# A graph network's edge loop: one own-computed edge tile per lap in place of three, shorter address lists, and the window ramp in SBUF

## The chip, the cores and the metric

The kernel runs on one core of a Trainium2 chip. The metric is the device time of one execution in microseconds (us). Of the kernel before it is 1872.18 us, the median of three runs that lie between 1870.85 and 1880.07.

## The reference, cut to what matters

A message-passing layer over 12500 nodes of 64 features and 200000 edges of 32 features. The edges are sorted by destination node.

```python
msg_in = jnp.concatenate([nodes[row], nodes[col], edge_features], axis=-1)
messages = relu(msg_in @ mW1 + mb1) @ mW2 + mb2
aggregated = jax.ops.segment_sum(messages, col, num_segments=nodes.shape[0])
upd_in = jnp.concatenate([nodes, aggregated], axis=-1)
upd = relu(upd_in @ uW1 + ub1) @ uW2 + ub2
out = layernorm(nodes + upd)
```

Here `row` is `src` (random) and `col` is `dst` (sorted). The first layer of the message network is linear ahead of its relu, so its three parts can be computed apart and added: one part from the source node, one from the destination node, one from the edge.

## The kernel before, in words

**Tables.** The kernel first multiplies all node rows with the source part of `mW1` and writes the result to DRAM as `src_table`, then does the same for the destination part (`dst_table`). GpSimd waits until `src_table` is stored before its first gather.

**The edge loop.** The edges are cut into tiles of 128, four tiles to a group, eight groups to a lap: 32 tiles a lap, 49 laps, of which the last has 7 groups. In all there are 391 groups. For each group g:

- GpSimd (`gather`, L305 to L317) fetches rows of `src_table` with one indirect DMA for each tile into `ag`. It may run at most eight groups ahead of the compute engines: it waits for `s_pre` of group g - 8.
- SP loads a window of 96 rows of `dst_table` (L329) and the edges' features (L323).
- VectorE makes a one-hot matrix `oh` (L402): it compares a ramp `iota` of 96 numbers with each edge's place in the window, for four tiles at once. Both inputs are broadcast to 128 x 384.
- TensorE transposes it (L338), ScalarE copies it to SBUF (L383), and TensorE multiplies destination window and edge features with it (L353).
- VectorE adds the gathered source part (`add_source`, L416), ScalarE applies the relu (L394), TensorE adds the rows of one destination up (L368, L372), and VectorE adds the window into the sums (`add_window`, L433 and L434).

**Own tiles.** Some tiles of a lap are not gathered. `OWN_OF` says how many in each of the eight groups of a lap: one each in groups 0, 2 and 5, so 3 of 32. For these the kernel fetches the feature columns of the source nodes itself from `xc`, which lies in SBUF: one copy of 64 x 4 bytes for each edge, at an address that is read from `own_list` into a register (L282). The 384 columns of a lap are spread evenly over its eight groups, `OWN_N` = 48 in each: `OWN_DVE` = 20 by VectorE (L290, in `own_columns`), the other 28 by ScalarE (L302). `DVE_AHEAD` and `ACT_AHEAD` = 12 say how many addresses each engine reads into registers ahead of its `add_source` or its relu; the rest is read behind it. TensorE then multiplies the own tile with `w_src` (L357), and the relu of such a group is in two parts (L391, L392). The copies of one lap are for the tiles of the next. The first lap has no own tiles.

**Order on VectorE in group g:** one-hot of group g + 2, register reads, `add_source` of g, register reads, `add_window` of g - 2, own copies, then in some groups a piece of the update.

**The update.** From lap 26 on (`UPD_LAP`), one chunk of 512 nodes a lap goes through the update network and the layer norm, in pieces between the groups (L749 to L841). Two chunks are left for after the last lap, and end the kernel. Three of these pieces read two SBUF tensors in one VectorE instruction: L770, L802 and L828.

Of the kernel before, what the change touches and what calls it, by code (L numbers as in the profile page):

```python
# [9 lines left out]
P = 128  # L10
# [12 lines left out]
WIN = 96  # L23
# [13 lines left out]
UPD_LAP = ITERS - CHUNKS + TAIL  # L37
TB = 4
TSTEPS = -(-BLOCKS // TB)
OWN_OF = (1, 0, 1, 0, 0, 1, 0, 0)  # L40
OWN_TILES = sum(OWN_OF)
OWN = OWN_TILES * P
OWN_N = OWN // UNROLL
OWN_DVE = 20
DVE_AHEAD = 12
ACT_AHEAD = 12
LIST = OWN // 2
XPARTS = 8
XP = NODES // XPARTS
# [7 lines left out]
def build(nc, x_rows, x_t, src_first, src_all, src_own, dst_groups, dst_tiles, edge_t,  # L57
# [12 lines left out]
    with ctx:  # L70
        def sb(name, shape, dt=f32):
            return ctx.enter_context(nc.sbuf_tensor(name, shape, dt))
# [19 lines left out]
        ident_bf = sb("ident_bf", [P, P], bf16)  # L92
        eps = sb("eps", [P, 1])
        iota_i = sb("iota_i", [P, WIN], i32)
        ones_bf = sb("ones_bf", [P, P], bf16)
        w_src = sb("w_src", [P, DH])
        b1_rows = sb("b1_rows", [P, DH])
# [11 lines left out]
        xc = sb("xc", [P, NODES])  # L109
# [42 lines left out]

        banks = [ctx.enter_context(nc.psum_tensor(f"bank{i}", [P, 512], f32)) for i in range(8)]
        ps_h, ps_o, ps_a = banks[0:2], banks[2:4], banks[4:6]
        iota = banks[6][:, 0:WIN]


        s_first = sem("s_first")
# [85 lines left out]
        def gathered_tiles(k):  # L244

            return TPG - OWN_OF[k]

        def has_own(k, lap):

            return OWN_OF[k] > 0 and not (isinstance(lap, int) and lap == 0)  # L250

# [25 lines left out]
        def own_places(et, k, lap, a, b):  # L277

            if a == b or isinstance(lap, int) and lap == ITERS - 1:
                return []  # L280
            at = k * OWN_N
            return nc.values_load_multi_w_load_instructions(  # L282
                own_list[0:1, at + a:at + b], engines=(et,), min_val=x_at, max_val=x_at + 4 * (N_NODES - 1),
                skip_runtime_bounds_check_because="the address of a node's column in xc")[1]

        def own_columns(k, a, places, copy, s_done):

            at = k * OWN_N + a
            for n, place in enumerate(places):
                done = copy(own_x[:, at + n:at + n + 1].bitcast(u8),  # L290
                            xc[0:D, :].bitcast(u8)[:, ds(place - x_at, 4)])
            if places:
                done.then_inc(s_done, 1)
# [5 lines left out]
        def own_columns_act(k, places):  # L299

            def copy(to, of):
                return nc.scalar.activation(to, of, ACT.Copy)  # L302
            own_columns(k, OWN_DVE, places, copy, s_own_act)

# [37 lines left out]
        def hidden(pe, g, k, lap):  # L342
# [7 lines left out]
            own = gathered_tiles(k) if has_own(k, lap) else TPG  # L350
            before_k = sum(OWN_OF[:k])
            for j in range(TPG):
# [24 lines left out]
        def copy_oh(g, k):  # L377

            act = nc.scalar
            q, r = k % 2, k % RING  # L380
            wait(act, s_oht_mm, g + 1)
            wait(act, s_h, g - RING + 1)
            act.activation(picks[0:WIN, r, :], ps_o[q][0:WIN, :], ACT.Copy).then_inc(s_oht, 1)  # L383

        def relu(g, k, lap):
            act = nc.scalar
            q = k % 2
            wait(act, s_pre, g + 1)
            if has_own(k, lap):
                at = gathered_tiles(k) * DH  # L390
                act.activation(hid[:, q, at:], ps_h[q][:, at:], ACT.Relu)  # L391
                act.activation(hid[:, q, 0:at], hid[:, q, 0:at], ACT.Relu).then_inc(s_relu, 1)  # L392
                return
            act.activation(hid[:, q, :], hid[:, q, :], ACT.Relu).then_inc(s_relu, 1)  # L394

        def one_hot(g, k):

            dve = nc.vector
            r = k % RING
            wait(dve, s_agg, g - RING + 1)  # L400
            grid = [P, TPG, WIN]
            dve.tensor_tensor(oh[:, r, :].rearrange("p (j w) -> p j w", w=WIN),  # L402
                              iota[:, None, :].to_broadcast(grid),
                              rel[:, ds(g * TPG, TPG)][:, :, None].to_broadcast(grid),
                              ALU.is_equal).then_inc(s_oh, 1)

        def add_source(g, k, lap):

            dve = nc.vector
            q = k % 2  # L410
            missing = G_END * TPG - T_END if isinstance(g, int) and g == G_END - 1 else 0
            wait(dve, s_gathered[k], gathered_of(k, lap) - 16 * missing)
            wait(dve, s_h, g + 1)
            wait(dve, s_agg, g - 1)
            w = (gathered_tiles(k) if has_own(k, lap) else TPG) * DH
            dve.tensor_tensor(hid[:, q, 0:w], ps_h[q][:, 0:w], ag[:, k, 0:w], ALU.add).then_inc(s_pre, 1)  # L416
# [131 lines left out]
        def exists(g):  # L548

            return not isinstance(g, int) or g < G_END  # L550
# [270 lines left out]
        def dve_normalize(c, v=None):  # L821
            dve = nc.vector
            y = blocks(rows_of(c))
            rstd, _, _, std = stats(c, v)
            dve.wait_ge(s_std, c + 1)
            dve.reciprocal(rstd, std).then_inc(s_rstd, 1)
            dve.wait_ge(s_rstd, c + 1)
            dve.tensor_tensor(y, y, rstd[:, :, None].to_broadcast([P, filled(c), D]), ALU.mult  # L828
                              ).then_inc(s_norm, 1)
# [167 lines left out]
        def _(act):  # L997
# [11 lines left out]
            def windowed():  # L1009
                dst_table_stored(act)  # L1010
                copy_oh(0, 0)

                def lap(i, c):
                    for k in range(UNROLL):
                        g = i * UNROLL + k
                        own_listed(act, k, i)
                        if exists(g + 1):
                            copy_oh(g + 1, (k + 1) % UNROLL)
                        places = own_places(ET.Activation, k, i, OWN_DVE, OWN_DVE + ACT_AHEAD)
                        if exists(g):  # L1020
                            relu(g, k, i)
                        places += own_places(ET.Activation, k, i, OWN_DVE + ACT_AHEAD, OWN_N)
                        own_columns_act(k, places)
                        if before(c) and k == 0:
                            act_square(c - 1)
                        elif before(c) and k == 2:
                            act_deviation(c - 1)
                        elif before(c) and k == 4:
                            act_store(c - 1)
                        elif c is not None and k == 5:  # L1030
                            act_relu(c)

                def finish(c):
                    act_square(c)
                    act_deviation(c)
                    act_store(c)
                laps(act, lap, open_update, finish, act_chunks)
# [10 lines left out]
        def _(dve):  # L1048
# [7 lines left out]
            dve.memset(ones_bf[:, :], 1.0)  # L1056
            dve.memset(src_idx[:, TILES:], 0).then_inc(s_const, 1)
            dve.wait_ge(s_iota, 3)
            dve.tensor_copy(iota, iota_i[:, :])
            dve.tensor_copy(trash_f[:, :], trash_i[:, :])  # L1060
            dve.tensor_copy(lag_f[:, :], lag_i[:, :]).then_inc(s_iotaf, 1)
            dve.wait_ge(s_ident, 2)
# [40 lines left out]
            def windowed():  # L1103
# [9 lines left out]
                def lap(i, c):  # L1113
# [4 lines left out]
                    for k in range(UNROLL):  # L1118
                        g = i * UNROLL + k
                        own_listed(dve, k, i)  # L1120
                        if exists(g + 2):
                            one_hot(g + 2, (k + 2) % UNROLL)
                        places = own_places(ET.DVE, k, i, 0, DVE_AHEAD)
                        if exists(g):
                            add_source(g, k, i)
                        places += own_places(ET.DVE, k, i, DVE_AHEAD, OWN_DVE)
                        if not (isinstance(g, int) and g < 2):
                            add_window(g - 2, (k - 2) % UNROLL, bases[k])
                        own_columns_dve(k, places)
                        if before(c) and k == 1:  # L1130
                            dve_variance(c - 1)
                        elif before(c) and k == 3:
                            dve_normalize(c - 1)
                        if c is not None and k == 1:
                            dve_c2(c)
                        elif c is not None and k == 3:
                            dve_stack(c)
                        elif c is not None and k == 7:
                            dve_center(c)
# [105 lines left out]
```

## Time and profile before

| what | value |
|---|---|
| profiled execution, its own time | 1872.18 us |
| its span, first to last instruction | 1870.4 us |
| median of three runs | 1872.18 us |
| gathers on GpSimd | 1419 |
| one-hots, groups | 391 |
| own copies on VectorE / ScalarE | 7680 / 10752 |
| own tiles | 144 |
| busy share PE / VectorE / ScalarE / GpSimd | 77% / 74% / 82% / 72% |

Busy shares are means over the whole span. What matters is which engine never waits for another. GpSimd's issue gap between gathers is not counted as busy. Start times are counted from the start of the span. The profiled execution is the one whose time equals the median, 1.8 us above its span.

### The profile page before, as it was taken

The page shows a single profiled execution, that of the slowest core. Times are in us where ns is not written, and L with a number is a line of the kernel's source. Part 1 is how long each engine was busy: PE and PEld are TensorE (multiplying, and loading weights), DVE is VectorE, ACT ScalarE, POOL GpSimd, SP SyncE. Part 2 cuts the span into 40 slices and gives each one's busy share as a digit, 9 for nine tenths or more (in the row PEclk, how much of TensorE's full clock was granted, in tenths as well). Part 3 has the DMA queues.
Part 4 walks back from the last instruction along what each step waited for, and adds up shares of the span by engine and source line. Part 5 has one row for each costly group of instructions (what it writes and reads, how often), then busy time and mean ns, then how long its engine had stood idle before and what let it go on. Part 6 is the DMA issues. An engine that isn't in the chain of part 4 may idle for free.

```text
span 1870.4 us, 55266 instructions
## 1 busy us (share of the span) xinstructions
PE 1437.6 (77%) x10368; PEld 1287.0 (69%) x10368; DVE 1381.8 (74%) x9522; ACT 1529.9 (82%) x11781; POOL 1347.6 (72%) x1432
## 2 busy tenths in 40 slices
PE   6677778778777878777777777777777777777776
PEld 6666677677666767766776777666666666676665
DVE  3488777777777777777777778777778778877885
ACT  3399988888888888888888888888888888888884
POOL 1677777777777777777777777777777777777771
PEclk8899887887878787788788778888778878887888
DMA  9933323332323333333332332332233323332331
GB/s 209 263 93 87 88 78 83 86 80 80 86 80 81 83 84 80 83 83 81 81 79 80 81 82 80 80 84 80 79 81 84 81 78 81 85 80 77 84 82 30
DMA packets 170541, 165.24 MB, mean 88 GB/s; under 512 B 70442, under 2 KB 134418, under 8 KB 170402
## 3 DMA queue, kind: packets, MB, share of 16 engines
q0 software_dynamic: 45408, 93.09, 19.1%
q1 hardware_dynamic: 111394, 64.42, 12.5%
q10 hardware_dynamic: 13698, 7.28, 1.8%
q8 instruction: 14, 0.23, 0.1%
q14 instruction: 27, 0.22, 0.0%
HBM read 148.25 MB, written 16.39 MB: 88 GB/s over the span
## 4 chain that ended last, share of the span: by engine, by line
POOL 35%; ACT 16%; issue 16%; PE 12%; DVE 10%; DMA 4%; ACTq 4%; DVEq 3%; POOLq 1%; SPq 0%
POOL ag L314 35%; ACT own_x L302 12%; PE bank L353 5%; ACTq L282 3%; DVE own_x L290 3%; DVE hid L416 2%; PE bank L368 2%; PE bank L749 2%; DMA src_table<-ag 2%; PE bank L762 1%; ACT hid L394 1%; DVEq L282 1%; ACT picks L383 1%; DMA dst_table<-hid 1%; DVE oh L402 1%
## 5 line engine op out<-in xcount | busy, mean ns | idle before, releaser
L314 POOL DMA_INDIRECT ag<-src_table,slot_idx x1419 | 1341.1, 945 | 481.1 <-issue 420.4
L302 ACT ACTIVATE own_x<-xc 64x4 uint8 x10752 | 1064.7, 190 | 101.5 <-issue 101.0
L353 PE MATMUL bank<-picked,picks 128*128 128x128 f32 x3128 | 548.0, 330 | 217.7 <-ACT picks L383 208.5
L353 PEld LDWEIGHTS bank<-picked,picks 128*128 128x128 f32 x3128 | 474.2, 232 | 250.8 <-ACT picks L383 159.5
L290 DVE COPY own_x<-xc 64x4 uint8 x7680 | 606.6, 190 | 12.0
L368 PE MATMUL bank<-oh,hid 128*128 128x96 f32 x3128 | 528.8, 324 | 24.7 <-DVE xc L434 23.8
L368 PEld LDWEIGHTS bank<-oh,hid 128*128 128x128 f32 x3128 | 483.7, 236 | 57.9 <-ACT hid L394 21.0
L416 DVE TENSOR_TENSOR hid<-bank,ag 128x512 f32<-128x512 f32 (+1 forms) x391 | 249.9, 639 | 290.7 <-DMA ag<-src_table,slot_idx 144.2
L402 DVE TENSOR_TENSOR oh<-bank,rel 128x384 f32<-128x384 f32 x391 | 217.9, 557 | 55.5 <-issue 28.7
L338 PE MATMUL bank<-ident_bf,oh 128*96 128x128 bf16 x1564 | 178.4, 244 | 88.2 <-DVE oh L402 86.1
L383 ACT ACTIVATE picks<-bank 96x512 f32<-96x512 f32 x391 | 224.7, 575 | 24.3 <-DMA dst_table<-picks 22.8
L394 ACT ACTIVATE hid<-hid 128x512 f32<-128x512 f32 x247 | 154.3, 625 | 100.2 <-DVE hid L416 100.2
L338 PEld LDWEIGHTS bank<-ident_bf,oh 128*96 128x96 bf16 x1564 | 132.3, 141 | 140.2 <-DVE oh L402 104.9
L372 PE MATMUL bank<-oh,ones_bf 128*128 128x96 bf16 x1564 | 150.0, 224 | 0.0
L433 DVE TENSOR_TENSOR agg_t<-bank,agg_t 128x96 f32 x391 | 100.6, 257 | 61.7 <-issue 32.5
L372 PEld LDWEIGHTS bank<-oh,ones_bf 128*128 128x128 bf16 x1564 | 138.3, 119 | 1.0
L434 DVE TENSOR_TENSOR xc<-bank,xc 64x96 f32 x391 | 102.2, 261 | 5.4
L391 ACT ACTIVATE hid<-bank 128x128 f32<-128x128 f32 x144 | 38.4, 267 | 64.3 <-DVE hid L416 59.6
L357 PE MATMUL bank<-w_src,own_x 64*128 64x128 f32 x288 | 84.9, 382 | 0.0
L392 ACT ACTIVATE hid<-hid 128x384 f32<-128x384 f32 x144 | 74.1, 514 | 0.0
L357 PEld LDWEIGHTS bank<-w_src,own_x 64*128 64x128 f32 x288 | 52.1, 226 | 21.9 <-issue 9.8
L762 PE MATMUL bank<-u,dst_i 128*128 128x64 f32 x196 | 29.1, 295 | 46.9 <-ACT dst_i L786 46.9
(62 smaller groups left out, 414.5 us busy)
## 6 DMA issues: line engine op xcount, KB each, us to landing
picks<-edge_t SPq DMA_DIRECT2D x391, 64.0 KB
ag<-src_table,slot_idx POOLq DMA_INDIRECT x1419
picked<-dst_table SPq DMA_DIRECT2D x391, 48.0 KB
src_table<-ag SPq DMA_DIRECT2D x25, 256.0 KB, 4.1
dst_table<-picks SPq DMA_DIRECT2D x17, 256.0 KB, 4.4
xc<-x_t ACTq DMA_DIRECT2D x8, 400.0 KB, 16.1
resid<-x_rows SPq DMA_DIRECT2D x24, 128.0 KB
out<-resid ACTq DMA_DIRECT2D x24, 128.0 KB
```

The lines of the kernel that those rows point to most:

```text
L290: done = copy(own_x[:, at + n:at + n + 1].bitcast(u8), xc[0:D, :].bitcast(u8)[:, ds(place - x_at, 4)])
L302: return nc.scalar.activation(to, of, ACT.Copy)
L314: pool.indirect_dma_start(out=ag[:, k, j * DH:(j + 1) * DH], out_offset=None, in_=src_table, in_offset=bass.IndirectOffsetOnAxis(ap=slot_i ...
L338: last = nc.tensor.matmul(ps_o[q][0:WIN, j * P:(j + 1) * P], half[:, j * WIN:(j + 1) * WIN], ident_bf[:, :], start=True, stop=True)
L353: last = nc.tensor.matmul(ps_h[q][:, j * DH:(j + 1) * DH], picks[:, r, j * P:(j + 1) * P], picked[:, r, :], start=True, stop=j < own)
L357: last = nc.tensor.matmul(ps_h[q][:, j * DH:(j + 1) * DH], own_x[:, (before_k + j - own) * P:(before_k + j - own + 1) * P], w_src[0:D, :], ...
L368: nc.tensor.matmul(ps_a[q][:, 0:WIN], hid[:, q, j * DH:(j + 1) * DH], oh[:, r, j * WIN:(j + 1) * WIN], start=(j == 0), stop=(j == TPG - 1))
L372: last = nc.tensor.matmul(ps_a[q][:, WIN:2 * WIN], ones_bf[:, :], half[:, j * WIN:(j + 1) * WIN], start=(j == 0), stop=(j == TPG - 1))
L383: act.activation(picks[0:WIN, r, :], ps_o[q][0:WIN, :], ACT.Copy).then_inc(s_oht, 1)
L394: act.activation(hid[:, q, :], hid[:, q, :], ACT.Relu).then_inc(s_relu, 1)
L402: dve.tensor_tensor(oh[:, r, :].rearrange("p (j w) -> p j w", w=WIN), iota[:, None, :].to_broadcast(grid), rel[:, ds(g * TPG, TPG)][:, :, ...
L416: dve.tensor_tensor(hid[:, q, 0:w], ps_h[q][:, 0:w], ag[:, k, 0:w], ALU.add).then_inc(s_pre, 1)
```

## The change

Own tiles are one a lap (in group 0) and not three. A lap's own list is then 128 edges, 16 for each group: eight on VectorE and eight on ScalarE, all of whose addresses are read ahead. The ramp `iota` of the one-hot lies in SBUF, where before it lay in a PSUM bank. The `list(...)` around the register reads changes no instruction.

```diff
-OWN_OF = (1, 0, 1, 0, 0, 1, 0, 0)
+OWN_OF = (1, 0, 0, 0, 0, 0, 0, 0)
 OWN_TILES = sum(OWN_OF)
 OWN = OWN_TILES * P
 OWN_N = OWN // UNROLL
-OWN_DVE = 20
-DVE_AHEAD = 12
-ACT_AHEAD = 12
+OWN_DVE = 8
+DVE_AHEAD = 8
+ACT_AHEAD = 8
...
+        iota = sb("iota", [P, WIN])
...
-        iota = banks[6][:, 0:WIN]
...
-            return nc.values_load_multi_w_load_instructions(
+            return list(nc.values_load_multi_w_load_instructions(
...
-            dve.tensor_copy(iota, iota_i[:, :])
+            dve.tensor_copy(iota[:, :], iota_i[:, :])
```

## Rows read from the trace of the kernel before

**Rows 1.** The page's busy times by engine: us, share of span, instructions.

```profile
PE 1437.6 (77%) x10368; PEld 1287.0 (69%) x10368; DVE 1381.8 (74%) x9522; ACT 1529.9 (82%) x11781; POOL 1347.6 (72%) x1432
```

**Rows 2.** The page's chain that ended last, by engine.

```profile
POOL 35%; ACT 16%; issue 16%; PE 12%; DVE 10%; DMA 4%; ACTq 4%; DVEq 3%; POOLq 1%; SPq 0%
```

**Rows 3.** All gathers, those from 57.6 to 999 us (ns min/median/max, starts), their waits.

```profile
L314 POOL DMA_INDIRECT ag<-src_table,slot_idx x1419: 940/944/1147, 56.3 to 1828.7; - x178
...
L314 POOL DMA_INDIRECT ag<-src_table,slot_idx x754: 940/944/961, 57.7 to 997.9; - x189
...
POOL ag L314 <- issue: 420.4, 1379, 0.3
```

**Rows 4.** Timeline, early gathers and VectorE's first own copies: start, duration in us.

```profile
57.70 0.94 POOL L314 DMA_INDIRECT ag<-src_table,slot_idx  x1 [0.30 <-issue]
58.95 0.95 POOL L314 DMA_INDIRECT ag<-src_table,slot_idx  x1 [0.30 <-issue]
...
90.24 0.90 DVE L290 COPY own_x<-xc 64x4 uint8 x11
```

**Rows 5.** VectorE's longest waits, 400 to 800 us, then 1100 to 1500 us: total, times, longest.

```profile
DVE hid L416 <- DMA ag<-src_table,slot_idx: 70.3, 75, 2.0
...
DVE hid L416 <- PE bank L353: 38.6, 19, 3.5
```

**Rows 6.** Costliest groups that the change touches: count, busy us, mean ns, idle before.

```profile
L302 ACT ACTIVATE own_x<-xc 64x4 uint8 x10752 | 1064.7, 190 | 101.5 <-issue 101.0
L290 DVE COPY own_x<-xc 64x4 uint8 x7680 | 606.6, 190 | 12.0
...
L357 PE MATMUL bank<-w_src,own_x 64*128 64x128 f32 x288 | 84.9, 382 | 0.0
```

**Rows 7.** Timeline around group 105: its last gather, its work on VectorE, group 106.

```profile
538.37 0.94 POOL L314 DMA_INDIRECT ag<-src_table,slot_idx  x1 [0.30 <-issue]
...
540.88 0.69 DVE L416 TENSOR_TENSOR hid<-bank,ag 128x512 f32<-128x512 f32 x1 [0.34 <-DMA ag<-src_table,slot_idx]
541.71 0.26 DVE L433 TENSOR_TENSOR agg_t<-bank,agg_t 128x96 f32 x1
...
542.11 0.94 POOL L314 DMA_INDIRECT ag<-src_table,slot_idx  x1 [0.30 <-issue]
542.27 1.56 DVE L290 COPY own_x<-xc 64x4 uint8 x20
...
543.87 0.56 DVE L402 TENSOR_TENSOR oh<-bank,rel 128x384 f32<-128x384 f32 x1
544.60 0.56 DVE L416 TENSOR_TENSOR hid<-bank,ag 128x384 f32<-128x384 f32 x1 [0.18 <-DMA ag<-src_table,slot_idx]
```

**Rows 8.** Timeline at 1136 us: a two-input SBUF instruction, a gather, the next gather.

```profile
1136.38 0.43 DVE L828 TENSOR_TENSOR resid<-resid,stat 128x256 f32 x1 [0.16 <-DVE stat L826]
1136.48 1.14 POOL L314 DMA_INDIRECT ag<-src_table,slot_idx  x1 [0.30 <-issue]
...
1137.93 0.94 POOL L314 DMA_INDIRECT ag<-src_table,slot_idx  x1 [0.30 <-issue]
```

**Rows 9.** Timeline at 1270 us: the same pair of kinds.

```profile
1270.16 0.42 DVE L802 TENSOR_TENSOR resid<-resid,stat 128x256 f32 x1
1270.35 1.06 POOL L314 DMA_INDIRECT ag<-src_table,slot_idx  x1 [0.30 <-issue]
```

**Rows 10.** Timeline at 1081 us: the same pair of kinds, the gather first.

```profile
1081.51 0.94 POOL L314 DMA_INDIRECT ag<-src_table,slot_idx  x1 [0.31 <-issue]
1081.54 0.43 DVE L802 TENSOR_TENSOR resid<-resid,stat 128x256 f32 x1
```

**Rows 11.** Timeline at the end: last gather, `add_source` of the last group, last issued store.

```profile
1828.71 0.94 POOL L314 DMA_INDIRECT ag<-src_table,slot_idx  x1 [0.30 <-issue]
...
1849.23 0.69 DVE L416 TENSOR_TENSOR hid<-bank,ag 128x512 f32<-128x512 f32 x1 [1.19 <-PE bank L353]
...
1867.11 0.38 ACTq L841 DMA_DIRECT2D out<-resid  x1
```

**Rows 12.** Granted TensorE clock near the end: window, length, PE busy, clock, DMA share, GB/s.

```profile
1855.00:1860.00 5.00, 4.49 (x8) 0.66 0.11 26
```

More of the change, by code:

```diff
@@ L281, in own_places @@
             at = k * OWN_N
-            return nc.values_load_multi_w_load_instructions(
+            return list(nc.values_load_multi_w_load_instructions(
                 own_list[0:1, at + a:at + b], engines=(et,), min_val=x_at, max_val=x_at + 4 * (N_NODES - 1),
-                skip_runtime_bounds_check_because="the address of a node's column in xc")[1]
+                skip_runtime_bounds_check_because="the address of a node's column in xc")[1])
         def own_columns(k, a, places, copy, s_done):
```

## The prediction

> **What bounds the kernel now.** I read the page's busy times first [rows 1]. By them ScalarE, with 82%, looks like the bound and GpSimd, with 72%, like the least loaded. The page's chain of work says something else: GpSimd has the largest part of it, 35%, ahead of ScalarE's 16% [rows 2]. The gathers settle it. From 57.7 to 997.9 us there are 754 of them [rows 3], so 753 intervals of 940.2 / 753 = 1.249 us: 0.94 us of work and 0.30 us in which GpSimd waits for nothing that the profile shows. That "issue" gap stands before 1379 of the 1419 gathers and is never longer than 0.3 us [rows 3]. Over the whole kernel the mean is (1828.7 - 56.3) / 1418 = 1.250 us. So GpSimd never stops between its first gather and its last: the stream of gathers is a rod of 1772 us, and the kernel is the time ahead of it (56.3), the rod, and what comes after the last start (1870.4 - 1828.7 = 41.7).
>
> The other engines are near the bound without being it. In the first half VectorE's `add_source` waits for gathered rows, 75 times between 400 and 800 us. In the second half, where the update is mixed in, its longest wait is for TensorE and the gathers have left the list's top [rows 5]. There compute falls behind, at most by the eight groups that GpSimd may run ahead. This shows at the end: the last gather starts at 1828.71, and the last group's `add_source` at 1849.23, 20.5 us later [rows 11], where in the first half it is 540.88 - 538.37 = 2.5 us later [rows 7].
>
> **The change part by part.** *More gathers.* Two tiles more are gathered in each of 47 full laps and two in the last: 96 gathers. At 1.249 us each that is +119.9 us on the rod. Nothing hides it, because the rod has no gaps.
>
> *Fewer own copies.* ScalarE loses 20 of 28 in each of 384 groups, 7680 copies; 7680 x 1064.7 / 10752 = 761 us of busy time [rows 6]. VectorE loses 4608: 4608 x 606.6 / 7680 = 364 us. TensorE loses 192 of 288 matmuls of L357, 57 us, and their weight loads. The relus of 96 groups are no longer split. All of this lies beside the rod and shortens it by nothing. It does shorten what comes after. A gathered group now takes 31/8 x 1.249 = 4.84 us on GpSimd where it took 4.53, and the compute engines, which managed a group in 4.53 + 18 / 184 = 4.63 us with the update among it (they lost 18 us on the rod over 23 laps of 8 groups), have 20 x 0.099 = 2.0 us of ScalarE's work less a group. In the last lap, which copies nothing, they were quick enough to shrink the lag already. So compute should keep up to the end, and the last `add_source` should start 2.5 us after the last gather: 20.5 - 2.5 = -18.0 us.
>
> *The register reads.* Eight addresses are read at once, and the second read between `add_source` and `add_window` is gone. On the path this is nothing, since both engines now wait for gathers.
>
> *The ramp in SBUF.* By itself the one-hot costs the same or slightly less on VectorE, which has slack. But it now reads two SBUF tensors, and instructions of that kind do something to gathers. In the trace there are three such lines in the update. L828 starts 0.10 us before a gather and ends 0.33 us after the gather's start: that gather takes 1.14 us instead of 0.94, and the next starts 1.45 us later instead of 1.25 [rows 8]. L802, begun 0.19 before a gather and ended 0.23 after its start, makes it 1.06 [rows 9]. L802 begun 0.03 us after a gather's start costs nothing, 0.94 [rows 10]. All three fit one rule: if such an instruction is under way when a gather starts, the gather is delayed until it ends, less 0.13 us. The Trainium skill says the same in words ("SBUF — State Buffer", section "Who interferes with whom"): a VectorE instruction with two SBUF inputs contends with a GpSimd instruction that reads SBUF, and the one that came first holds the port. The rows agree with it, and add that only the gather's start is exposed. By the page alone, with a hold at any overlap, a one-hot could cost its whole 0.56 us, 391 x 0.56 = 219 us and 2193 us in all; by the rows the most is the 141 us below.
>
> What a one-hot costs hangs on where it falls between gathers. In a gather-bound group this is fixed, since `add_source` starts at a fixed time behind a gather. In group 105 it is 2.51 us after the last gather, in 106 it is 2.49 [rows 7]. The one-hot starts 2.99 us after `add_source`, with 20 copies of 1.56 us in between. With 8 copies it is 0.94 less, and up to 0.14 less again for the register read that stood between L416 (ended 541.57) and L433 (541.71): 1.91 to 2.05. So it starts 4.4 to 4.56 us behind a gather. The fourth gather after that starts 4 x 1.249 = 5.00 us behind it, and the one-hot, 0.56 long, ends at 4.98 to 5.12, that is 0.02 before to 0.12 after. The rule's 0.13 is just not reached. A landing 0.1 us later or an update piece in the way takes it over. Bounds: nothing, if all miss; (0.56 - 0.13 - 0.07) = 0.36 us each at worst, 391 x 0.36 = 141 us. At random phases a hit has chance 0.36 / 1.25 = 0.29 and mean 0.18, 391 x 0.052 = 20 us. As the phase lies at the edge, I take 0.02 us each, between nothing and random: +8 us.
>
> Ahead of the rod, the own list's tables shrink to a third, from 384 to 128 addresses a lap; I take nothing for it, an estimate of at most 1 us. After the rod, TensorE's granted clock is 0.66 already between 1855 and 1860 us [rows 12], so a lower one there has little left to cost; with more waiting in the last lap I allow up to 3 us and take nothing.
>
> **Sum,** against the profiled execution's 1872.2, which is also the median: 1872.2 + 119.9 - 18.0 + 8 = 1982.1 us.
>
> **The rivals.** *The one-hots hit the gathers' starts.* Everything as above, but phases fall badly. For it: the estimated end is within hundredths of the edge, and each delay sits on the rod. Against: a delay moves the rod and the next `add_source` together, so no drift into a worse phase. Without locks the sum is 1974.1; at random phases it is 1974.1 + 20 = 1994 us, at worst 1974.1 + 141 = 2115 us.
>
> *No lock at all for the one-hot* (its second input is one short ramp read over and over): 1872.2 + 119.9 - 18.0 = 1974 us, less up to 3 us for shorter tables and for the 2 us of delays that the old rod holds.
>
> *Compute does not catch up.* For it: TensorE waits more and may be granted a lower clock, and TensorE is the longest wait of the second half [rows 5]. Against: ScalarE and VectorE have some 2 and 0.9 us a group less, and GpSimd leaves 0.3 us a group more. The lag then stays: 1872.2 + 119.9 = 1992, plus the locks 2000 us.
>
> *Faster: the copies were what made gathers slow.* The mechanism is on VectorE: 20 one-source copies a group from SBUF to SBUF would hold GpSimd back while it writes a gather's descriptors. With 8 copies the interval would shrink. It decides from the point where 1515 gathers fit: (1872.2 - 1.8 - 56.3 - 2.5 - 21.2 ) / 1515 = 1.182 us, 5% below 1.249. At 1.15 us the time would be 1.8 + 56.3 + 1742 + 24 = 1824 us. Against it stands a plain row: between 57.70 and 58.95, before VectorE's first own copy at 90.24, the interval is 1.25 us too [rows 4]. The Trainium skill (same page, section "SBUF: two separate sides") names this trap for fp32 copies on VectorE beside DMAs issued from GpSimd; the trace disagrees for copies as small as these. I give it 2%.
>
> **How the numbers follow.** Forecast with a lock cost from 2 to 14 us, 1974 to 1988: 0.60. No lock or nearly, 1968 to 1974: 0.12. Worse phases, 1988 and up: 0.16, of which half stay under 2003. Lag kept, 1992 to 2000: 0.09. Faster: 0.02. Something that makes it come out even: 0.01. The range from 1971 to 2003 leaves out about 0.08 above, 0.03 for the faster cases and even ones, and some 0.04 below 1971. A measurement of this kernel tells a change of about 0.5%, 9 us; all cases but the last two are slower by more: slower 0.97, same 0.01, faster 0.02.
>
> **What would show it right or wrong.** Right: 1515 gathers, most of them 1.249 us apart; a last gather near 1949 to 1957 us; `add_source` waiting for gathered rows in both halves, and about 2.5 us behind the last gather at the end; ScalarE's busy share near (1530 - 761) / 1980 = 39%; gathers longer than 0.96 us at one-hots that began just before them, with 8 us in sum over 0.94. Wrong: an interval other than 1.25 us where no one-hot is near; a last `add_source` 20 us behind; gathers of 1.1 us and more in every group; or a first gather moved by more than 1 us.

## The result, and the profile after

The changed kernel takes 1991.68 us (median of 4 runs, 1991.02 to 1992.42), the kernel before 1871.51 us beside it. It is slower by the factor 1.0632, interval 1.06 to 1.0663, where 1982.1 us were forecast. The profiled execution took 1988.3 us, with a span of 1986.6 us; the accounts below are made in that span.

First the page of the changed kernel: busy times, and the chain that ended last.

```profile
PE 1425.8 (72%) x10176; PEld 1300.5 (65%) x10176; DVE 1006.4 (51%) x4914; ACT 783.1 (39%) x4005; POOL 1451.5 (73%) x1528
...
POOL 71%; issue 24%; DMA 2%; POOLq 1%; PE 1%; DVE 0%; SPq 0%; ACT 0%; ACTq 0%; DVEq 0%
```

ScalarE fell from 82% to 39% [rows 1] and the kernel got slower. GpSimd's part of the chain doubled, from 35% [rows 2] to 71%, and with its issue gaps it is nearly the whole kernel. All its gathers, and what GpSimd waited for:

```profile
L314 POOL DMA_INDIRECT ag<-src_table,slot_idx x1515: 940/944/1525, 55.6 to 1961.1; - x190
...
POOL ag L314 <- issue: 461.1, 1513, 0.3
```

96 gathers more than in [rows 3], the same median of 944 ns, and again no wait but the 0.3 us gap. What is new is the longest one, 1525 ns. VectorE's longest wait, from 400 to 800 us and from 1100 to 1500 us:

```profile
DVE hid L416 <- DMA ag<-src_table,slot_idx: 198.6, 82, 2.9
...
DVE hid L416 <- DMA ag<-src_table,slot_idx: 159.5, 72, 3.0
```

In [rows 5] the second stretch was led by TensorE; now both halves wait for gathered rows. The timeline at the end, to be held against [rows 11]:

```profile
1961.05 0.94 POOL L314 DMA_INDIRECT ag<-src_table,slot_idx  x1 [0.31 <-issue]
...
1964.64 0.69 DVE L416 TENSOR_TENSOR hid<-bank,ag 128x512 f32<-128x512 f32 x1 [3.66 <-DMA ag<-src_table,slot_idx]
...
1983.23 0.38 ACTq L841 DMA_DIRECT2D out<-resid  x1
```

The last `add_source` starts 3.6 us behind the last gather, where it was 20.5 us. So the 116.2 us by which the span grew are:

| part | before | after | difference |
|---|---|---|---|
| first gather starts | 56.29 | 55.65 | -0.6 |
| gathers at 1.249 us | 1418 intervals | 1514 intervals | +119.9 |
| gathers' delays beyond that | 1.3 | 14.4 | +13.1 |
| last gather to last `add_source` | 20.5 | 3.6 | -16.9 |
| from there to the end | 21.2 | 21.9 | +0.7 |

The delays are what the intervals hold beyond 1.249 us each. In the trace 68 gathers take 30 ns or more over 944 ns, and all but four of them lie beside a one-hot (the four are the first gather of all, and three beside the update's own two-input instructions). Such a pair in the update's laps:

```profile
1188.71 0.56 DVE L402 TENSOR_TENSOR oh<-iota,rel 128x384 f32<-128x384 f32 x1 [0.99 <-issue]
1188.84 1.24 POOL L314 DMA_INDIRECT ag<-src_table,slot_idx  x1 [0.30 <-issue]
...
1190.39 0.94 POOL L314 DMA_INDIRECT ag<-src_table,slot_idx  x1 [0.30 <-issue]
```

The one-hot starts 0.13 us before the gather and ends 0.42 us after the gather's start. The gather takes 0.30 us longer, that is 0.42 less 0.13, as [rows 8, 9] had it. The same gathers as one group (count, busy us, mean ns, idle time before) give the sum in one row:

```profile
L314 POOL DMA_INDIRECT ag<-src_table,slot_idx x1515 | 1444.9, 954 | 509.6 <-issue 461.1
```

1444.9 - 1515 x 0.944 = 14.7 us. This subtraction is the measure of delay in what follows.

### The profile page after: what moved, and what is told of

It reads as the page before. It is cut to its first block, busy times and chain, and to the rows that moved or that the text cites. A ratio compares the mean times of both kernels' runs of the same rounds, so it can differ in the third digit from the quotient of the medians.

```text
span 1986.6 us, 41684 instructions
## 1 busy us (share of the span) xinstructions
PE 1425.8 (72%) x10176; PEld 1300.5 (65%) x10176; DVE 1006.4 (51%) x4914; ACT 783.1 (39%) x4005; POOL 1451.5 (73%) x1528
## 4 chain that ended last, share of the span: by engine, by line
POOL 71%; issue 24%; DMA 2%; POOLq 1%; PE 1%; DVE 0%; SPq 0%; ACT 0%; ACTq 0%; DVEq 0%
POOL ag L314 71%; DMA src_table<-ag 1%; DMA xc<-x_t 1%; POOLq L233 1%; PE bank L477 0%; POOLq L311 0%; DMA ag<-src_table,slot_idx 0%; DMA own_columns<-resid 0%; SPq L506 0%; PE bank L749 0%; PE bank L755 0%; PE bank L368 0%; POOLq L894 0%; ACT ag L488 0%; DVE resid L828 0%
## 5 line engine op out<-in xcount | busy, mean ns | idle before, releaser
L314 POOL DMA_INDIRECT ag<-src_table,slot_idx x1515 | 1444.9, 954 | 509.6 <-issue 461.1
L394 ACT ACTIVATE hid<-hid 128x512 f32<-128x512 f32 x343 | 215.8, 629 | 998.0 <-DVE hid L416 998.0
L353 PEld LDWEIGHTS bank<-picked,picks 128*128 128x128 f32 x3128 | 510.2, 247 | 14.0 <-issue 12.4
L302 ACT ACTIVATE own_x<-xc 64x4 uint8 x3072 | 328.3, 189 | 0.0
L290 DVE COPY own_x<-xc 64x4 uint8 x3072 | 303.3, 180 | 12.0
L402 DVE TENSOR_TENSOR oh<-iota,rel 128x384 f32<-128x384 f32 x391 | 213.0, 545 | 45.5 <-issue 26.1
L383 ACT ACTIVATE picks<-bank 96x512 f32<-96x512 f32 x391 | 224.5, 574 | 23.1 <-DMA dst_table<-picks 22.5
L357 PE MATMUL bank<-w_src,own_x 64*128 64x128 f32 x96 | 27.6, 377 | 113.8 <-ACT own_x L302 93.9
L357 PEld LDWEIGHTS bank<-w_src,own_x 64*128 64x128 f32 x96 | 17.8, 231 | 122.7 <-DVE own_x L290 122.7
L755 PE MATMUL bank<-xc,u 128*128 (+2 forms) x50 | 45.5, 1014 | 8.4 <-DVE xc L778 8.4
L477 PE MATMUL bank<-w_src,xc 128*128 128x128 f32 x200 | 29.0, 317 | 16.2 <-DMA xc<-x_t 9.0
```

What stands on the lines that cost most here:

```text
L290: done = copy(own_x[:, at + n:at + n + 1].bitcast(u8), xc[0:D, :].bitcast(u8)[:, ds(place - x_at, 4)])
L314: pool.indirect_dma_start(out=ag[:, k, j * DH:(j + 1) * DH], out_offset=None, in_=src_table, in_offset=bass.IndirectOffsetOnAxis(ap=slot_i ...
L353: last = nc.tensor.matmul(ps_h[q][:, j * DH:(j + 1) * DH], picks[:, r, j * P:(j + 1) * P], picked[:, r, :], start=True, stop=j < own)
```

## The experiments

The first four ran on one chip, where the kernel before took 1869.5 us.

### The ramp back in PSUM

```diff
-        iota = sb("iota", [P, WIN])
+        iota = banks[6][:, 0:WIN]
...
-            dve.tensor_copy(iota[:, :], iota_i[:, :])
+            dve.tensor_copy(iota, iota_i[:, :])
```

> The changed kernel with the one-hot's ramp back in PSUM, all else as changed. Theory (one-hots with two SBUF inputs delay gathers that start beside them; in the profile of the changed kernel 68 gathers are delayed by 30 ns or more, 14.6 us in sum, nearly all beside a one-hot): 1991.7 less about 13 us, so 1977 to 1981 us; gathers longer than 0.96 us only beside the update's two-input instructions, some 2 us in sum. Rival (the delays are the gathers' own, or come from the DMA queues): 1990 to 1993 us and as many long gathers.

1974.39 us, 1.0554 times the kernel before (1.0513 to 1.0596). Its gathers:

```profile
L314 POOL DMA_INDIRECT ag<-src_table,slot_idx x1515 | 1430.8, 944 | 510.0 <-issue 460.4 <-DMA src_table<-ag 48.4 <-DVE hid L416 0.9
```

1430.8 - 1515 x 0.944 = 0.6 us of delay where the changed kernel has 14.7. Five of the six gathers delayed by over 30 ns lie beside L828, and the sixth is the first of all. So the ramp in SBUF costs 1991.7 - 1974.4 = 17 us across the two measurements, or (1.0632 - 1.0554) x 1870 = 15 us by the ratios. The other part of the change costs the rest: 1974.4 is 0.3 us from the prediction's sum without locks, 1872.2 + 119.9 - 18.0 = 1974.1. That close a match is partly luck: from the 1869.5 us of the kernel before on this chip the same sum gives 1971.4, 3 us less than measured.

### The ramp in SBUF, with three own tiles

```diff
+        iota = sb("iota", [P, WIN])
...
-        iota = banks[6][:, 0:WIN]
...
-            dve.tensor_copy(iota, iota_i[:, :])
+            dve.tensor_copy(iota[:, :], iota_i[:, :])
```

> The kernel before with only the ramp moved to SBUF (three own tiles a lap, 20 and 28 copies). Theory: in its first half the one-hots start 0.5 us after a gather and miss the gathers' starts, except in group 7 of each lap, where they start about 0.1 us before one and cost 0.3 us, 8 us in all; in the second half they fall anywhere, 9 us on the gathers, of which the lag of the compute engines hides a part. 1876 to 1890 us, best 1882. Rival (a ramp in SBUF is only a quicker read, the one-hot 545 ns instead of 558): 1868 to 1872 us.

1911.07 us, 1.0209 times the kernel before (1.0168 to 1.0251), so 39 to 42 us slower: the right side, but over three times the 10 to 12 us of the best estimate.

```profile
L314 POOL DMA_INDIRECT ag<-src_table,slot_idx x1419 | 1396.5, 984 | 481.6 <-issue 426.5 <-DMA src_table<-ag 49.3 <-DVE hid L416 5.5
```

1396.5 - 1419 x 0.944 = 57.0 us of delay. In the span, the last gather starts at 1884.6 instead of 1828.7, 55.9 us later, and the last group's lag falls from 20.5 to 3.0 us, which gives 17.5 us back. In the trace the first half (gathers before 1000 us) holds 27.8 us of delay beside one-hots, and the rest of the kernel 28.5, where 8 and 9 were expected. The hits of group 7 came as expected: 24 of them, 8.2 us. What I missed is that they move what follows. In the kernel before, the one-hot of group 0 starts 0.37 us behind a gather; here it starts 0.16 us sooner, the hit of group 7 has moved the gathers by 0.35, and it starts 0.14 us before one: 0.37 - 0.16 - 0.35 = -0.14. So group 0 hits too, and pushes some of groups 1 and 2 onto gathers: 53 hits in groups 0 to 2, 19.0 us. These sums fit that account; no run tries it by itself. Of the hits of the first half, 22 are of this kind, all in group 0, with 0.28 us each:

```profile
860.69 0.54 DVE L402 TENSOR_TENSOR oh<-iota,rel 128x384 f32<-128x384 f32 x1
...
860.83 1.22 POOL L314 DMA_INDIRECT ag<-src_table,slot_idx  x1 [0.30 <-issue]
```

The edit only moves the ramp. It makes each one-hot 17 ns quicker (541 ns at the median for 558) and the kernel 2% slower.

### Six more copies a group, with either ramp

```diff
+EXTRA = 6
...
+            for n in range(EXTRA if places else 0):
+                nc.vector.tensor_copy(spare[:, k * EXTRA + n:k * EXTRA + n + 1].bitcast(u8),
+                                      xc[0:D, :].bitcast(u8)[:, ds(places[0] - x_at, 4)])
             own_columns(k, 0, places, nc.vector.tensor_copy, s_own_dve)
```

With the ramp in SBUF:

> The changed kernel with six more 4-byte copies on VectorE in each group ahead of its own copies (into a spare tile that nothing reads), so that each one-hot starts 0.47 us later. Theory: in groups 1 to 6 of a lap the one-hot then starts 0.2 us before a gather and ends 0.3 us after the gather's start, costs that gather 0.2 us, 390 x 6/8 x 0.2 = 58 us more on the gathers: 2030 to 2070 us, best 2048. Rival (VectorE has over 2 us of slack a group, so six copies of 79 ns cost nothing): 1990 to 1993 us.

2055.27 us, 1.0985 times the kernel before (1.0928 to 1.1041). Nothing was added but 0.47 us a group on VectorE, which then was busy 57% of the time, and the kernel lost 64 us against the changed one in its own measurement. Its gathers as a group, and one pair of its timeline (lines are five higher than before):

```profile
L319 POOL DMA_INDIRECT ag<-src_table,slot_idx x1515 | 1512.4, 998 | 509.5 <-issue 460.6 <-DMA src_table<-ag 48.0 <-DVE hid L421 0.6
...
746.54 0.54 DVE L407 TENSOR_TENSOR oh<-iota,rel 128x384 f32<-128x384 f32 x1
746.58 1.32 POOL L319 DMA_INDIRECT ag<-src_table,slot_idx  x1 [0.30 <-issue]
...
748.20 0.94 POOL L319 DMA_INDIRECT ag<-src_table,slot_idx  x1 [0.30 <-issue]
```

1512.4 - 1515 x 0.944 = 82.2 us of delay, 67 more than in the changed kernel. 187 of the one-hots start 0.20 to 0.30 us before a gather, as expected, and delay it by 0.13 to 0.22 us, 31 us in all. The rest of the 82 us comes from closer hits, as in the pair shown, which ends 0.50 after the gather's start and costs 0.38; group 0 of the laps alone, which the expectation left out, has 20 us.

With the ramp in PSUM:

> The same six more copies in each group, with the ramp in PSUM. Theory: the shift costs nothing once the one-hot has a single SBUF input: the time of the changed kernel with the ramp in PSUM, 1977 to 1981 us. Rival (the six copies themselves hold the gathers back, by the port or by VectorE's time): as much above that as the other shifted kernel is above the changed one, 2030 us and more.

1983.42 us, 1.0601 times the kernel before (1.0546 to 1.0655), 9 us above the kernel without the six copies.

```profile
L319 POOL DMA_INDIRECT ag<-src_table,slot_idx x1515 | 1440.3, 951 | 509.5 <-issue 460.3 <-DMA src_table<-ag 48.0 <-DVE hid L421 1.2
...
1271.24 1.37 POOL L319 DMA_INDIRECT ag<-src_table,slot_idx  x1 [0.30 <-issue]
...
1271.38 0.41 DVE L775 TENSOR_TENSOR resid<-resid,c_rows 128x256 f32 x1
```

10.1 us of delay, and none of it comes from a one-hot: 252 one-hots are under way when a gather starts and end over 0.16 us behind it, and the longest delay among them is 0.01 us. With the same six copies and the ramp in SBUF there are 277 such one-hots, and all 277 gathers are late by over 0.03 us. It lies beside the update's two-input instructions (L775 and L807 there, L770 and L802 before), which the six copies had pushed onto gathers' starts. So the expectation missed 2 to 6 us, and these delays account for it: the same kind of instruction with two SBUF inputs, on another line.

### Three other chips

The other eight runs went to three other chips (four, two and two), where the kernel before took 2678, 2785 and 2660 us. They can't be held against the runs above, so each is told here beside the kernel before on its own chip. Each chip was measured once; whether it is the chip or its condition at that time that matters is not shown.

> The kernel before with two own tiles a lap (groups 0 and 4; 32 columns a group, 14 on VectorE and 18 on ScalarE), ramp in PSUM: 48 gathers more than before. Theory (time = start of the gathers + their number x 1.249 us + an end of about 25 us once the compute engines keep up): 1872 + 60 - 18 = 1914 us, 1908 to 1920. Rival (the gathers are not what bounds, the copies are): below 1872 us, since ten copies on ScalarE and six on VectorE are gone from each group.

```diff
-OWN_OF = (1, 0, 1, 0, 0, 1, 0, 0)
+OWN_OF = (1, 0, 0, 0, 1, 0, 0, 0)
...
-OWN_DVE = 20
+OWN_DVE = 14
```

2570.02 us, 0.9595 times the kernel before (0.9525 to 0.9665). Once more, on the next chip:

> The kernel with two own tiles a lap (32 columns a group, 14 and 18) and the ramp in PSUM once more, since on the chip of its first run all kernels, the kernel before too, took 1.4 to 2.2 times their usual time, with sequencers that got their instructions late. Theory (start + gathers x 1.249 us + an end of about 25 us): 1908 to 1920 us, best 1914. Rival (the copies bound): below 1872 us.

2628.25 us, 0.9437 times (0.94 to 0.9473). On these chips the rival's side comes out: fewer copies win. What differs is seen in TensorE's timeline, here of the changed kernel itself on the third chip:

```profile
1507.15 0.20 PE L372 MATMUL bank<-oh,ones_bf 128*128 128x96 bf16 x1 [0.41 <-issue]
1508.58 0.24 PE L372 MATMUL bank<-oh,ones_bf 128*128 128x96 bf16 x1 [1.22 <-issue]
1509.99 0.24 PE L372 MATMUL bank<-oh,ones_bf 128*128 128x96 bf16 x1 [1.18 <-issue]
```

These are matmuls of one group that wait for nothing between them, and there are 1.2 us of "issue" between one and the next. The engines sit idle for no reason that the profile gives. GpSimd is then no longer the one that never waits. Waits in that profile (total, times, longest):

```profile
ACT picks L383 <- remote: 702.1, 146, 10.6
...
POOL ag L314 <- DVE hid L416: 573.5, 178, 26.6
...
POOL ag L314 <- issue: 422.6, 1330, 3.1
```

GpSimd waits 574 us for VectorE's sums, and nothing in [rows 3] answers to that. The longest wait of all is ScalarE's copy of the transposed one-hot; "remote" is a releaser that the profile can't place, but in the kernel L383 waits only for counts that TensorE raises. So these waits lead back to TensorE.

ScalarE shows gaps of its own ahead of its own copies. On the first of these chips they are 701 us of "issue" in the kernel with three own tiles and half the rows (told below) and 631 us with two own tiles; on the third chip, in the changed kernel with one, there are none. In the trace of the kernel before it is 101 us [rows 6]. The first of these, as total, times and longest:

```profile
ACT own_x L302 <- issue: 700.6, 1170, 1.2
```

On these chips more own copies thus come with more idle time than where the prediction's rows were taken. That fits the turned sign; no run tries it by itself. The changed kernel on the third:

> The changed kernel itself, since on two of three chips the kernel before took 2678 and 2785 us instead of 1870. If this chip gives the kernel before 1870 us: 1989 to 1993 us again. If it gives it 2650 us or more: theory (there the engines' sequencers get their instructions late, so time follows the number of own copies and register reads; two own tiles a lap were already 4 to 6 per cent faster than three): the changed kernel is the faster one, 2000 to 2500 us. Rival (all engines are slowed alike): 1.06 times the kernel before.

2557.44 us, 0.9605 times the kernel before (0.9542 to 0.9667), faster as the theory had it, though above its 2000 to 2500 us: the same edit that costs 6% where the kernel before takes 1870 us gains 4% on this chip. That sequencers get their instructions late, as the expectations say, no profile here shows; what it shows are the gaps.

> The kernel before with gathers of 64 rows instead of 128, which leaves the source part of every second half tile ungathered; the number of gathers is the same. Theory A (the 1.249 us are GpSimd's cost of an instruction, whatever it fetches): the interval stays 1.25 us and the time 1872 us. Theory B (they are a cost of each row): the interval falls to about 0.8 us and the compute engines bound the kernel, at 4.4 to 4.6 us a group: 1800 to 1865 us. Both are open; the transfers themselves do not bound, with the DMA engines 31 per cent busy.

```diff
-                    out=ag[:, k, j * DH:(j + 1) * DH], out_offset=None, in_=src_table,
-                    in_offset=bass.IndirectOffsetOnAxis(ap=slot_idx[:, par, c:c + 1], axis=0),
+                    out=ag[0:P // 2, k, j * DH:(j + 1) * DH], out_offset=None, in_=src_table,
+                    in_offset=bass.IndirectOffsetOnAxis(ap=slot_idx[0:P // 2, par, c:c + 1], axis=0),
```

2772.49 us, 1.0351 times the kernel before (1.028 to 1.0422). This time says nothing of gathers, since they don't bound there. But where two gathers follow at once, the cost of one can be read all the same:

```profile
1001.89 0.90 POOL L314 DMA_INDIRECT ag<-src_table,slot_idx  x1 [0.30 <-issue]
1003.09 0.90 POOL L314 DMA_INDIRECT ag<-src_table,slot_idx  x1 [0.30 <-issue]
1004.30 0.90 POOL L314 DMA_INDIRECT ag<-src_table,slot_idx  x1 [0.30 <-issue]
```

1.205 us for 64 rows beside 1.249 us for 128. Theory A holds: the cost is nearly all the instruction's, and a row is under a nanosecond of it, (1.249 - 1.205) / 64. The 128-row gathers of the changed kernel on another of these chips show the usual 1.249 us where they follow at once.

The last three give the copies other counts, and none was tried on a chip like the first ones.

> The kernel before with four own tiles a lap (groups 0, 2, 4, 5; 64 columns a group, 30 on VectorE and 34 on ScalarE), ramp in PSUM: 48 gathers fewer. Theory: the gathers stop being the bound and the compute engines take over. ScalarE has six copies more a group, 0.6 us, and VectorE ten, 0.8 us, on a group of 4.5 to 4.6 us: 5.1 to 5.4 us a group, 1980 to 2080 us, with gaps between gathers that wait for the sum of an earlier group. Rival (the gathers bound alone): 1872 - 60 = 1812 us.

```diff
-OWN_OF = (1, 0, 1, 0, 0, 1, 0, 0)
+OWN_OF = (1, 0, 1, 0, 1, 1, 0, 0)
...
-OWN_DVE = 20
-DVE_AHEAD = 12
+OWN_DVE = 30
+DVE_AHEAD = 14
```

4103.59 us, 1.5321 times (1.522 to 1.5421). Its expectation of 1980 to 2080 us was for a chip like the first, and stays untried.

> The kernel before with its 48 copies a group split 24 and 24 (before: 20 on VectorE, 28 on ScalarE). Theory: the gathers stay as they are, 1772 us from first to last start; in the second half, where ScalarE's copies are the largest part of the chain of work, the compute engines lose less, and the 20.5 us between the last gather and the last group shrink: 1855 to 1870 us, best 1863. Rival (VectorE's part grows as much as ScalarE's shrinks, 0.32 against 0.40 us a group): 1872 us or a few more.

```diff
-OWN_DVE = 20
+OWN_DVE = 24
```

2744.7 us, 1.0243 times (1.0184 to 1.0302). With 22 in place of 24, on two chips:

> The kernel before with its 48 copies a group split 22 and 26 (before: 20 on VectorE, 28 on ScalarE). Theory: the gathers stay as they are; in the laps with the update ScalarE's copies are the largest part of the chain, so the compute engines lag less at the end, and the 20.5 us between the last gather and the last group shrink by 5 to 15 us: 1857 to 1867 us. Rival (VectorE is as close to its limit as ScalarE): 1870 us or more.

3156.17 us, 1.1337 times (1.1302 to 1.1372).

> The kernel before with its 48 copies a group split 22 and 26, once more. On a chip that gives the kernel before 1870 us: gathers unchanged, a shorter lag at the end, 1857 to 1867 us; rival: 1870 us or more. On a slow chip: slower than the kernel before, as in its first run there, 1.13 times.

3136.12 us, 1.1782 times (1.1722 to 1.1842). Whether these splits shorten the lag was not settled. The two splits run the same number of instructions as the kernel before, 55266, but their pages show another instruction traffic. The page's row of the instruction queue (packets, MB, share), for 22 and 26, then for 24 and 24, then for four own tiles:

```profile
q14 instruction: 148, 1.21, 0.1%
```

```profile
q14 instruction: 127, 1.04, 0.1%
```

```profile
q14 instruction: 472, 3.87, 0.3%
```

The kernel before has 27 such packets, the one with two own tiles 24, the changed one 19. All three kernels with more than a hundred are slower than the kernel before on their chip (24 and 24 by only 2%), and the two with fewer packets than it are faster. That the packets are the cause was not tried.

## Why the prediction was right, and where it was off

**The bound.** Right. 1418 and then 1514 intervals of 1.249 us, with no wait beyond the 0.3 us gap in either kernel. 96 more gathers cost 119.9 us, and with the ramp in PSUM the whole sum came out to 0.3 us, or to 3 us by the kernel before on that chip.

**Fewer own copies.** Right as an account: 761 us off ScalarE's busy time were forecast and 747 measured (1529.9 - 783.1), and it brought nothing but the lag. That was to fall by 18.0 us and fell by 16.9. The last group's rows take 3.6 us from the gather's start to `add_source`, not the 2.5 us of the groups in the middle; with the ramp in PSUM it was 3.3.

**The ramp in SBUF.** The mechanism was right, and the term mis-sized: +8 us were taken, +13.1 is what the span shows, and 15 to 17 is what the ramp alone costs. The step that failed is the phase, in two ways. In the gather-bound groups the one-hot starts 1.78 us behind `add_source`, not 1.91 to 2.05, so nearly all miss: all hits before 1000 us cost 2.0 us together. 212 of the 391 one-hots start 0.50 to 0.65 us behind a gather, out of harm. A group of the first half, to be held against [rows 7]:

```profile
538.42 0.69 DVE L416 TENSOR_TENSOR hid<-bank,ag 128x512 f32<-128x512 f32 x1 [2.67 <-DMA ag<-src_table,slot_idx]
...
539.59 0.95 DVE L290 COPY own_x<-xc 64x4 uint8 x8
539.60 0.94 POOL L314 DMA_INDIRECT ag<-src_table,slot_idx  x1 [0.30 <-issue]
...
540.21 0.54 DVE L402 TENSOR_TENSOR oh<-iota,rel 128x384 f32<-128x384 f32 x1
...
540.85 0.94 POOL L314 DMA_INDIRECT ag<-src_table,slot_idx  x1 [0.30 <-issue]
```

And in the update's laps the one-hots behind the pieces of groups 1 and 7 hit: behind group 1 in 21 of 23 laps, with 0.30 to 0.46 us each, behind group 7 in 9, with 0.29 to 0.31 us. With some grazes behind group 3 that is about 12 us. The prediction names "an update piece in the way" and counts nothing for it by itself. So it is luck that the term came out near its size: it came from another place than the one it was worked out from.

**The sum.** Against the forecast of 1982.1 us the profiled execution is 6.2 us longer, of which the delays have 5.1 and the lag 1.1. The other 3.4 us up to the median of 1991.7 lie between the profiled execution and the rest.

**"Begun after a gather's start it costs nothing".** Too strong, and with it the bound of 0.36 us a hit. The prediction shows one pair for it [rows 10]. In the changed kernel one-hots begun 0.02 us behind a gather's start, by their rows, cost nothing or 0.44 us:

```profile
92.59 0.95 POOL L314 DMA_INDIRECT ag<-src_table,slot_idx  x1 [0.30 <-issue]
92.61 0.57 DVE L402 TENSOR_TENSOR oh<-iota,rel 128x384 f32<-128x384 f32 x1 [0.33 <-PE bank L372]
...
1116.37 0.40 DVE L770 TENSOR_TENSOR resid<-resid,c_rows 128x256 f32 x1
...
1116.68 1.38 POOL L314 DMA_INDIRECT ag<-src_table,slot_idx  x1 [0.30 <-issue]
1116.70 0.54 DVE L402 TENSOR_TENSOR oh<-iota,rel 128x384 f32<-128x384 f32 x1
```

What goes with the difference is what VectorE did just before. The first one-hot starts after a gap. The second one's row starts 0.07 us before the row ahead of it (L770) ends, and the gather is held until 0.13 us before the one-hot's end. In the traces of the changed kernel, of the two shifted ones and of the ramp in SBUF with three own tiles, 122 two-input instructions start up to 0.16 us behind a gather's start and overlap the row ahead of them, mostly of own copies or of the update: 121 of these gathers are late, by up to 0.58 us. 84 start there after a gap: none is late. Why the overlap decides is open.

**The rivals.** "No lock" is refuted by the kernel with the ramp in PSUM (17 us less, and no gather late beside a one-hot), "compute does not catch up" by the 3.6 us. "The one-hots hit the gathers' starts" has the right mechanism, though for few one-hots. "Copies made gathers slow" is refuted too: the interval is 1.249 us with 8, 14 and 20 copies on VectorE.

**What stays open.** The runs without the profiler took 1991.0 to 1992.4 us, the profiled one 1988.3. Why it is 3 us quicker I can't say. And the sum holds where GpSimd never waits. On three other chips it waited, and the sign turned; why the engines have gaps there is not known. No row of the kernel before could show that.

## What to carry to other kernels

Look for the engine whose gaps are constant, not for the busiest one. An engine that issues one instruction every 1.249 us without ever waiting is the bound at 72% busy, and work taken from the others buys only the lag at the end. Where such an engine is GpSimd with indirect DMAs, count instructions, not rows, and keep VectorE's instructions with two SBUF inputs away from the gathers' starts: leave one input in PSUM, since otherwise even a shift within VectorE's idle time can cost. And an edit that trades instructions against gathers should be timed on more than one chip.

## What the runs showed of the hardware that I had not expected

- A gather of 64 rows takes GpSimd 1.205 us, one of 128 rows 1.249 us.
- A VectorE instruction with two SBUF inputs that is under way when a gather starts delays it until 0.13 us before its own end. One whose row starts up to 0.16 us behind the gather's start does the same, by up to 0.58 us, if that row overlaps the one ahead of it (121 of 122), and costs nothing after a gap (84 of 84). With one input in PSUM it never did (252 one-hots in one run). Six 4-byte copies a group that only shifted the one-hots cost 64 us.
- The kernel before took 1870 us in the first measurement and on the chip of the first four runs, and 2660 to 2785 us on three others, with gaps of 1.2 us between matmuls that wait for nothing (seen in the changed kernel) and 701 us of such gaps ahead of ScalarE's own copies (seen with half the rows). The order of two kernels is not the same on all chips: 1.0632 in the first measurement, 0.9605 on another chip. The cause is open.
